# A transformer tower on one Trainium2 core: where VectorE makes the table of looked-up experts in the first expert stage

## The reference

```
route   = softmax(x @ router_w + router_b)
max_ind = argmax(route);  max_prob = max(route)
for e in range(8):
    mask = (max_ind == e)
    out += mask * ((silu(x @ w1[e]) * (x @ w2[e])) @ w3[e])        # hidden width 512
out = bf16(out) * max_prob
```

## Time and profile before

| | |
|---|---|
| median of 3 runs | 354.21 us (353.32 to 358.28) |
| the profiled execution | 355.75 us, its span 354.0 us |
| granted TensorE clock | 1.00 of full speed over the span |
| first expert stage, from the ranks to the last pair | about 98 to 150 us of the span |

### The profile page before, as it was taken

The page is one execution under the profiler, slowest core; times in us unless marked ns, Lnnn a source line. Parts: engine busy times, 40 slices in busy tenths (PEclk is TensorE's granted clock), DMA queues, the critical chain, the costliest instruction groups (busy, mean ns, idle before and its releaser), DMA issues.

```text
span 354.0 us, 6894 instructions
## 1 busy us (share of the span) xinstructions
PE 330.6 (93%) x2609; PEld 257.3 (73%) x2624; DVE 184.5 (52%) x512; ACT 137.3 (39%) x287; POOL 92.7 (26%) x124
## 2 busy tenths in 40 slices
PE   4999999989987999889898998998999999999996
PEld 1999995635652545456676857677999999999995
DVE  2798587767562343278977625582124221621225
ACT  2999421782421222248982134321221221221320
POOL 8099824000014411104051020005233233222110
PEclk9999999999999999999999999999999999999999
DMA  6954138996979796170069991202499999999222
GB/s 210 412 97 111 12 101 246 276 257 183 250 268 375 206 251 176 32 200 2 1 179 289 247 251 37 76 3 74 97 286 280 290 255 266 253 257 258 65 74 89
DMA packets 31746, 64.57 MB, mean 182 GB/s; under 512 B 10817, under 2 KB 17506, under 8 KB 31714
## 3 DMA queue, kind: packets, MB, share of 16 engines
q1 hardware_dynamic: 29506, 59.38, 61.8%
q0 software_dynamic: 1920, 4.56, 4.7%
q10 hardware_dynamic: 288, 0.20, 0.2%
HBM read 54.74 MB, written 4.65 MB: 168 GB/s over the span
## 4 chain that ended last, share of the span: by engine, by line
PE 81%; DVE 7%; ACT 3%; DMA 3%; issue 2%; POOL 1%; another core or an unknown queue 0%; SPq 0%; DVEq 0%; ACTq 0%; POOLq 0%
PE ps L1905 12%; PE ps L1632 12%; PE ps L1930 10%; PE ps L1624 7%; PE ps L1917 7%; PE ps L1690 4%; PE ps L2029 3%; PE ps L1994 3%; PE ps L1696 2%; PE ps L2004 2%; PE ps L1773 2%; DMA xg<-token_x,src_id 2%; DMA xw<-in_xw 2%; PE ps L1845 2%; PE ps L1882 1%
## 5 line engine op out<-in xcount | busy, mean ns | idle before, releaser
L691 POOL DMA_INDIRECT xg<-token_x,src_id x22 | 21.5, 976 | 119.9 <-DVE src_id L1361 76.8
L1624 PE MATMUL ps<-busy 128*128 128x512 bf16 x164 | 46.5, 392 | 6.0 <-POOL ident L601 4.5
L1390 DVE TENSOR_TENSOR ht<-sg,ps 128x384 f32<-128x384 f32 (+1 forms) x48 | 23.8, 509 | 49.7 <-ACT sg L909 45.0
L1905 PE MATMUL ps<-xgt,wup 128*128 128x128 f32 x384 | 45.6, 275 | 1.6 <-ACT xgt L900 1.6
L1905 PEld LDWEIGHTS ps<-xgt,wup 128*128 128x128 f32 x384 | 44.8, 192 | 2.1 <-issue 2.1
L1632 PE MATMUL ps<-weff,xp 128*128 128x193 f32 x240 | 41.9, 338 | 0.9 <-ACT xp L752 0.9
L1632 PEld LDWEIGHTS ps<-weff,xp 128*128 128x128 f32 x240 | 41.2, 198 | 2.0 <-issue 2.0
L909 ACT ACTIVATE sg<-ps 128x384 f32<-128x384 f32 (+1 forms) x48 | 21.0, 455 | 50.0 <-PE ps L1917 33.0
L1930 PE MATMUL ps<-wdn,ht 128*128 128x192 f32 x192 | 35.2, 334 | 0.0
L698 POOL DMA_INDIRECT token_y<-ysb,row_id x20 | 19.7, 986 | 54.9 <-ACT ysb L916 54.5
L1930 PEld LDWEIGHTS ps<-wdn,ht 128*128 128x128 f32 x192 | 30.8, 190 | 1.8
(11 more groups left out here) (355 smaller groups left out, 576.5 us busy)
## 6 DMA issues: line engine op xcount, KB each, us to landing
w<-in_m_w SPq DMA_DIRECT2D x24, 384.0 KB, 7.8
wup<-in_m_w SPq DMA_DIRECT2D x16, 576.0 KB
wup<-in_m_w SPq DMA_DIRECT2D x48, 192.0 KB
wdn<-in_m_w SPq DMA_DIRECT2D x16, 576.0 KB
w<-in_m_w SPq DMA_DIRECT2D x36, 128.0 KB, 7.3
xw<-in_xw SPq DMA_DIRECT2D x2, 784.0 KB, 11.3
wall<-in_w_sh SPq DMA_DIRECT2D x2, 768.0 KB
token_y<-busy SPq DMA_DIRECT2D x2, 480.0 KB, 4.1
```

The source lines that it names most:

```text
L691: g.indirect_dma_start(xg[:, j, :], None, token_x[m], bass.IndirectOffsetOnAxis(ap=src_id[:, j:j + 1], axis=0))\
L1390: v.tensor_tensor(ht[:, j % 2, s, 0:half], sg[:, s, 0:half], ups, ALU.mult)\
L1624: mm(ps[:, bank, :], busy[:, 0:P], busy[:], start=True, stop=True)
L1905: mm(ps[:, 2 * s + g, c * P:c * P + P], up[:, col:col + P], xgt[:, 0, j * P:j * P + P], start=(c == 0), stop=False)
```

## The change

In the first expert stage (m = 0) the call of `looked_up()` moves from behind `base_e` to behind the last `at_r`, just ahead of the wait for `p_inv`. The second stage, in which the table was already made further down, is as before.

```diff
                 link(v.tensor_tensor_scan(base_e[:, 1:E], minus[:], over_e[:, 0:E - 1], E - 1.0, ALU.add, ALU.add))
-                if m == 0:
-                    looked_up()
                 link(v.scalar_tensor_tensor(out=rank_b[:], in0=ranks, scalar=1.0 / L,
...
                 for i in range(kt):
                     v.tensor_scalar(at_r[:, i, :], neg_r[:], slot_r[:, i // TT, i % TT:i % TT + 1], None,
                                     ALU.is_equal).then_inc(S["v_inv"], 1)
+                if m == 0:
+                    looked_up()
                 dve.wait_ge(S["p_inv"], m + 1)
                 v.tensor_copy(src_id[:, 0:n], ps[:, 5, 0:n]).then_inc(S["v_src"], 1)
```

## The result

The changed kernel took 359.28 us (median of 4 executions, 356.29 to 361.6), the kernel before 354.28 us (353.32 to 358.28). The ratio is 1.0162, with a 95% interval of 1.0113 to 1.0211. A second measurement gave 1.0146 (1.0081 to 1.0211). So the change costs about 5 us. The forecast was 356.3 us, with a range up to 358.2. It had the direction and the place, and less than half of the size.

What follows compares the result with a forecast made beforehand. TensorE, busy 93% of 354.0 us, was taken as the bound, with table, copies and loads a second chain. The last pair starts 2.05 us later, the 0.55 us gain waited away: 354.21 + 2.05 = 356.3 us, range 354.0 to 358.2.

Steps and rivals of the forecast that it cites:

- The removal: On VectorE, `rank_b` takes the place of `teb`, so TensorE's first tile and the gathers come 0.55 us earlier.
- The cover: VectorE's idle time of 0.94 us before `src_id` hides the three moved instructions, with 0.4 us left.
- The delay of the table: The table `te`, which SyncE reads before issuing copies, ends at 103.60 instead of 99.85: 3.75 us later.
- The chain behind it: Table, SyncE's copies, loads, TensorE's last pair: no room to catch up, so the delay reaches the last pair.
- the landing: Last weights land at about 139.1 us before (stragglers 140.3); with the delay 143.4 was taken, last pair +2.05 us.
- 4.1 us: Delay of the loads' end: 3.75 us from the table plus GpSimd's transfers of 0.15 and 0.24 us.
- The wait: TensorE arrives at the last pair at 140.80 and stands still for 2.6 us until the weights land at 143.4.
- the last weights would be in time: Rival at the last pair: weights land before TensorE arrives, the 0.55 us gain stands, 353.7 us; chance 0.15.
- gathers that find emptier queues: Same rival's second half: up to 1.88 + 0.20 us more of TensorE's idle time at the gathers goes, 351.6 us.
- The straggler's case: Rival: one DMA engine trails at the loads' end, last pair +3.0 to +3.7 us, 357.2 to 357.9 us; chance 0.2.
- A load stream of 14 us: Estimate by the skill's bandwidth rule: loads end near 134 us even before, so the late table costs nothing; not adopted.
- Theory A: From the experiments: late table delays copies and loads, the last pair waits for its weights, and TensorE's clock falls behind that wait.

Runs made afterwards that it cites:

- short loads: Changed kernel without the w3 loads of half tiles 12 to 15: 354.3 us, ratio 0.9979; the same edit on the kernel before: 354.96 us, ratio 1.0008.
- late SyncE: Kernel before, VectorE's list untouched, but SyncE also waits for the last list factor before it reads the table: 360.97 us, ratio 1.0229.
- table in the middle: Against the kernel before, the table is made behind `one_first`, the first tile's permutation: 354.26 us, ratio 1.0005.
- interleaved kernel: Kernel before with the table's instructions placed between those of the ranks, and the first `rank_b` instruction ahead of `base_e`: 356.19 us, ratio 1.0034.

## Why the prediction was wrong

**What held.** The removal: the first tile 0.53 us earlier (forecast 0.55). The cover: 0.40 us of VectorE's idle time left ahead of `src_id` (0.4). The delay of the table as SyncE felt it: the first copy 3.76 us later (3.75). The chain behind it, and the place where it comes back to TensorE: the last pair, and nowhere earlier. The short loads and the late SyncE show this chain to be the cause, each from its own side.

**The first mis-sized term: the landing.** I took 139.3 us for the landing before, near the row for most DMA engines, let the streams end 4.1 us later and had the last pair start at 143.4. What the pair waits for is the last packet. In the changed kernel the last packet of queue 1 began at 141.95 to 142.00 and the pair started 0.66 to 0.71 us behind it (0.53 to 0.73 in the six profiles in which the pair waits). In the kernel before it began at 139.85 to 139.90, so by the same distance the pair could have started at 140.56, and its slack was 0.8 us, where 139.3 gave 2.05. So the landing stood 1.26 us too early in my sum. The delay itself was slightly over-sized: counted from the fill work, the last packet came 3.97 us later, 0.13 less than my 4.1. 2.05 + 1.26 - 0.13 = 3.18 us, as measured. The kernel with the table in the middle checks it: last packet about 1.5 us late, less 0.8 of slack, 0.65 measured.

The 4.1 us came out nearly right partly by luck. The first load was 4.64 us late and the last transfer was issued 4.65 us late, since the copies, from their first issue to the first load, took 17.66 us in place of 16.78, where I had allowed 0.39 us for both streams together. From the last issue to the last packet it was then 7.75 us in place of 8.43. GpSimd's transfers do not explain the longer copies: with the table in the middle its sixth gather (115.72) and first scatter (117.03) were also ahead of the copies' end (119.3), and the same stretch took 16.57 us. It was 17.7 to 18.2 us in all six profiles with a first copy at 6.1 us and 16.6 to 17.0 in the other six. The cause stays open.

The wait, forecast at 2.6 us, was 3.90, because the pair started later and because TensorE also arrived earlier, by 0.9 us in place of 0.55: the first gathered rows held it for 1.33 us in place of 1.88.

**The step that was missing: what a longer wait does to the clock.** The prediction priced the wait by its length alone. Before, TensorE stood still for 1.88 us in this stage and its clock stayed at 1.00. I did not ask what 2.6 us or more would do, a length for which this stage has no row. In the profiles with 3.90, 3.88 and 3.80 us the clock fell to 0.50 and the stretch from the last pair to the end of the stage took 1.6 to 1.7 us more than before, while at 1.41, 0.99 and 0.85 us it stayed. The Trainium skill, Perfetto Trace Analysis, section Matmul Optimizations, says that power scales with how much the engine is used and that matmuls should run back to back. The trace agrees: behind the 3.90 us the same eight matmuls took 3.22 us against 1.89. Together the two terms give 3.18 + 1.68 = 4.86 us of stage.

That the medians differ by nearly the same, 5.0 us, is partly luck. Two of the four executions show a clock of 0.994 and 0.995, about that of one such loss, and took 357.24 and 356.29 us, 2 to 3 above the median before. The other two show 0.981 and 0.991 and took 361.33 and 361.6, so they lost more clock than that. The median lies between the pairs.

**The rivals.** That the last weights would be in time was wrong in this kernel: they were not. Its second half, gathers that find emptier queues, came true by some 0.35 us of its 2.08. The straggler's case, with a chance of 0.2, was the right one for the start of the last pair (+3.0 to +3.7, measured +3.18) and low for the time, 357.2 to 357.9 us, by the same missing clock. Its reason is not shown: in the changed kernel no packet of an instruction queue moved between 139 and 142 us, and queue 1 had its stragglers there all the same.

**A slip beside the sum.** A load stream of 14 us from 118.1 us on ends near 132 us, not near 134. The forecast does not rest on it.

**What stays open.** The loss of clock in the state-space stage is not explained. Theory A needs no such loss for the 4.86 us of the stage, and the counts of executions are too small to say whether the change, or fill work, makes it more frequent.

## What to carry to other kernels

An instruction that costs 0.2 us can be the trigger of a chain of 40 us on another engine. Before moving it off one path, follow its readers to the end and compare the slack there with the move. When a wait is what you forecast, price the clock behind it too: look for the longest gap of TensorE that kept its clock, and treat a longer one, or several close together, as unpriced. And when a wait ends with a transfer, read the last packet of its queue and not the end of the full stretch: here the last two packets came about 1 us behind the others. Where two chains on one engine both wait for their own results, their instructions can be interleaved almost for free.

## What the hardware showed that I had not expected

- TensorE's gap did not have to be long by itself. In the interleaved kernel two gaps, 1.14 and 1.85 us with work between them, were followed by a granted clock of 0.50, while the 1.88 and 0.20 us before were not.
- An independent VectorE instruction placed in the shadow of a linked one starts 0.08 to 0.13 us behind it (97.51 and 97.59, 97.92 and 98.05 above), where a linked one of this size starts 0.20 to 0.24 us behind. The three instructions of the table, 0.55 us of path before, then cost nearly nothing: the first tile began at 2.11 us, at 2.23 with the table moved away.
- The rate of the copies' stretch was 381 GB/s before and 361 GB/s changed, at shares of 0.98 and 0.94, with one more gather and a scatter of GpSimd in the second. The middle table's copies had both as well and were not longer than before.
